# Gated delta-rule attention and experts on one core: keys and queries stored as feature rows by the projections

## The reference

```python
q = (x @ Wq).reshape(B, T, H, DK);  k = (x @ Wk)...;  v = (x @ Wv)...
x1, x2 = x[..., :d], x[..., d:]                       # d = DK // 2
rotary = concatenate([x1 * c + x2 * s, -x1 * s + x2 * c])
qr = l2norm(rotary(q, cos, sin)) * scale              # one set of angles per head and mode
kr = l2norm(rotary(k, cos, sin))
def step(S, inp):                                     # scanned over T, for every mode, batch and head
    q_t, k_t, v_t, b_g, b_beta = inp
    S = S * exp(b_g)[..., None, None]
    kv = einsum('mbhk,mbhkv->mbhv', k_t, S)
    dv = (v_t[None] - kv) * b_beta[..., None]
    S = S + k_t[..., :, None] * dv[..., None, :]
    o_t = einsum('mbhk,mbhkv->mbhv', q_t, S)
    return (S, o_t)
o = einsum('tmbhv,hm->bthv', ys, softmax(mode_logits))
x = x + (o * gate).reshape(B, T, H * DV) @ Wo
x = x + ffn(layernorm(x))                             # grouped top-2 of 8 experts
```

## Time and profile before

| | us |
|---|---|
| three timed runs | 4,367.66, 4,371.86, 4,394.44 (median 4,371.86) |
| the profiled execution (its span) | 4,385.0 |
| PE, DVE, ACT, POOL busy | 3,813.9, 3,552.6, 2,905.5, 380.0 |
| projections, tables | 14.9 to 274.6, 275 to 351 |
| recurrence, experts | 351 to about 3,890, 3,893 to 4,385 |

### The profile page before, as it was taken

The page is one execution under the profiler, slowest core; times in us unless marked ns, Lnnn a source line. Parts: engine busy times, 40 slices in busy tenths (PEclk is TensorE's granted clock), DMA queues, the critical chain, the costliest instruction groups (busy, mean ns, idle before and its releaser), DMA issues. The chain is left out here.

```text
span 4385.0 us, 193447 instructions
## 1 busy us (share of the span) xinstructions
PE 3813.9 (87%) x85713; PEld 3121.1 (71%) x85713; DVE 3552.6 (81%) x6909; ACT 2905.5 (66%) x9768; POOL 380.0 (9%) x220
## 2 busy tenths in 40 slices
PE   5513898999999999998999899999998999979999
PEld 2203787788778878777877778777777787766666
DVE  5676898888889988888898889889898988835665
ACT  5743677777677777777776767777677777744443
POOL 1230010000001000000000001000000000000000
PEclk8756899999899999999999989999999999989999
DMA  4664122222222222222221222232222222121110
GB/s 115 166 173 118 49 57 76 57 57 62 70 57 57 69 69 60 62 53 68 57 66 48 75 57 57 59 77 65 53 58 68 66 56 61 45 67 32 34 34 8
DMA packets 311716, 289.21 MB, mean 66 GB/s; under 512 B 137816, under 2 KB 250336, under 8 KB 308832
## 3 DMA queue, kind: packets, MB, share of 16 engines
q1 hardware_dynamic: 310880, 276.83, 24.5%
HBM read 215.92 MB, written 60.82 MB: 63 GB/s over the span
## 5 line engine op out<-in xcount | busy, mean ns | idle before, releaser
L922 DVE TENSOR_TENSOR run_EL<-run_XL 128x30 f32<-128x30 f32 (+14 forms) x1920 | 643.4, 335 | 66.0
L923 DVE TENSOR_TENSOR run_XL<-run_XL,run_EL 128x30 f32<-128x30 f32 (+14 forms) x1920 | 637.3, 332 | 66.0
L1059 PE MATMUL run_SP<-run_KP 64*32 64x128 f32 x8192 | 581.4, 283 | 21.7 <-DVE run_KP L909 12.2
L992 POOL TENSOR_TENSOR run_DB<-run_DB,run_below 128x1024 f32<-128x1024 f32 x128 | 306.5, 2395 | 3213.9 <-DVE run_KP L909 1758.5
L795 ACT ACTIVATE run_DB<-run_DB,run_col 128x64 f32<-128x64 f32 x2048 | 541.4, 350 | 4.7 <-POOL run_DB L992 1.0
L885 DVE TENSOR_TENSOR run_SC<-run_SP,run_DB 128x512 f32<-128x512 f32 x512 | 341.0, 685 | 248.9 <-ACT run_DB L795 156.3
L1059 PEld LDWEIGHTS run_SP<-run_KP 64*32 64x32 f32 x8192 | 426.5, 111 | 94.5 <-issue 68.1
L802 ACT ACTIVATE run_KD<-run_PR,run_col 128x64 f32<-128x64 f32 x2048 | 481.9, 329 | 17.0 <-PE run_PR L1078 9.1
L808 ACT ACTIVATE run_R<-run_KS,run_col 128x64 f32<-128x64 f32 x1792 | 417.1, 325 | 83.2 <-PE run_KS L1086 83.0
L1063 PE MATMUL run_SP<-run_KP 64*32 64x64 f32 x8192 | 413.9, 231 | 8.6 <-issue 8.6
L815 ACT ACTIVATE run_Sdec<-run_S,run_decay 128x64 f32<-128x64 f32 x1536 | 416.3, 372 | 0.0
(11 more groups left out here) (200 smaller groups left out, 7523.7 us busy)
## 6 DMA issues: line engine op xcount, KB each, us to landing
run_DB<-G_s SPq DMA_DIRECT2D x512, 128.0 KB, 2.9
run_EG<-EG_s SPq DMA_DIRECT2D x128, 512.0 KB, 6.7
KQ_s<-proj_win SPq DMA_DIRECT2D x32, 768.0 KB, 7.5
run_win<-KQ_s SPq DMA_DIRECT2D x64, 384.0 KB
run_tab<-TAB_s SPq DMA_DIRECT2D x64, 256.0 KB, 7.0
run_V<-V_s SPq DMA_DIRECT2D x128, 128.0 KB, 3.1
V_s<-proj_vv SPq DMA_DIRECT2D x64, 128.0 KB, 3.1
TAB_s<-tab_tab SPq DMA_DIRECT2D x64, 128.0 KB, 2.4
```

The costliest lines, as they stand in the source:

```text
L922: v.link(dve.tensor_tensor(e, bcast(XL[:, r + 1:, r], 2, done), bcast(XL[:, r, 0:done], 1, rows), ALU.mult))
L923: less = dve.tensor_tensor(XL[:, r + 1:, 0:done], XL[:, r + 1:, 0:done], e, ALU.subtract)
L1059: pe.matmul(out[64 * e:64 * e + C, p].rearrange("p (z u) i -> p z (u i)", z=2), KP[f, key, p, t0:t1], KP[f, kq, p, t0:t0 + SPAN], start=Tr ...
```

## The change

- **Projections.** `win`, its negated columns and POOL's program are gone. DVE writes the normalised keys and queries into `unit` (two batches deep) with as many multiplications as before. Two batches later, `flush` transposes two heads per tile on PE (8 transposes of 128 x 128), ACT copies one of the heads from PSUM into `kqF` and DVE the other; one store of 2 MB a batch puts `kqF` into `KQ_s`, now by feature rows. The loop over batches has two more turns, for the flushes of the last two. V goes out in 2 stores a batch, G and EG in 3. The PSUM banks of q, k and v become a ring of three.
- **Tables.** A third plane holds the negative sines: one more ACT instruction and 4 more stores per head (96 in all).
- **Recurrence.** The four turns on PE and ACT's four copies are gone. `kqT` holds two sequences and is loaded from `KQ_s` by six DMAs per sequence (1 MB), at the head of SP's step. The minus of the rotation comes from the table's third plane. V is read in runs of 64 floats instead of 512. The pipeline starts one step later (-2 instead of -3). Keys 2 and 3 stand in other places on PE; keys 4 to 7 and the exponentials of "next" on ACT. merge(0,1) waits for the last step's merges instead of the turns; DVE's rotations wait for the load.

```diff
-    KQ_s = dram("KQ_s", (H, B, 128, NT, 2 * WIN))
-    V_s = dram("V_s", (H, B, SPAN, SUPER, DV))
+    KQ_s = dram("KQ_s", (B, 2 * DK, H, T))
+    V_s = dram("V_s", (B, SPAN, NT, 2, H, DV))
...
-    TAB_s = dram("TAB_s", (H, 2, 2, HALF, PAIRS, T))
+    TAB_s = dram("TAB_s", (H, 3, 2, HALF, PAIRS, T))
...
-            for b in range(B + 1):
+            for b in range(B + 2):
                 for i in range(NT):
                     if b < B:
                         tile(b, i)
-                    if b:
+                    if 1 <= b <= B:
                         after(b - 1, i)
+                    if b >= 2:
+                        flush(b - 2, i)
...
-                    for i in range(NT):
-                        sp.dma_start(KQ_s[:, b, :, i, :].rearrange("h p e -> p h e"), win[:, i, :, :]).then_inc(put_k, 16)
...
+                    if b >= 2:
+                        sp.wait_ge(fill_a, H // 2 * (b - 1))
+                        sp.wait_ge(fill_v, H // 2 * (b - 1))
+                        sp.dma_start(KQ_s[b - 2], kqF[:, b % 2]).then_inc(put_k[b % 2], 16)
...
+                def flush(b, i):
+
+                    if i == 0:
+                        pe.wait_ge(k_unit, b + 1)
+                        pe.wait_ge(q_unit, b + 1)
+                    for u, filled in enumerate((fill_a, fill_v)):
+                        h = 2 * i + u
+                        if H * b + h >= 2:
+                            pe.wait_ge(filled, H // 2 * b + i)
+                        for t in range(NT):
+                            last = pe.transpose(FB[u][:, 128 * t:128 * t + 128],
+                                                unit[:, b % 2, t, h].rearrange("p z f -> p (z f)"), ident[:, :])
+                        last.then_inc(pe_f, 1)
...
+                    act.copy(kqF[:, b % 2, 2 * i, :], FB[0][:, :]).then_inc(fill_a, 1)
...
+                    dve.tensor_copy(kqF[:, b % 2, 2 * i + 1, :], FB[1][:, :]).then_inc(fill_v, 1)
...
-                            for k in range(2):
+                            for k in range(3):
                                 sp.dma_start(TAB_s[h, k, e, :, q::2, :], tab[at:at + 32, u, k]).then_inc(put[u], 16)
...
+                    act.activation(tab[:, u, 2], ang[:, u], ACT.Sin, scale=-1.0).then_inc(done, 1)
...
-        STEPS = range(-3, NSEQ)
+        STEPS = range(-2, NSEQ)
...
-                     ["turn 0"], ["keys 2"], ["turn 1"], ["keys 3"], ["next 1"], ["turn 2"], ["next 2"], ["turn 3"]]
...
+                     ["keys 2"], [], ["keys 3"], [], ["next 1"], [], ["next 2"], []]
...
+                def load_kq(n):
+
+                    both = KQ_s[n % B, :, n // B, :].rearrange("(z f) t -> f z t", z=2)
+                    for e in range(2):
+                        rows = slice(64 * e, 64 * e + DK)
+                        sp.dma_start(kqT[rows, n % 2, 0::2, :], both).then_inc(l_kq, 16)
+                        for half in range(2):
+                            at, other = 64 * e + HALF * half, HALF * (1 - half)
+                            sp.dma_start(kqT[at:at + HALF, n % 2, 1::2, :], both[other:other + HALF]).then_inc(l_kq, 16)
...
-                                sp.dma_start(tab[at:at + HALF, k], TAB_s[h, k, e]).then_inc(l_tab, 16)
+                                sp.dma_start(tab[at:at + HALF, k], TAB_s[h, k + (k and half), e]).then_inc(l_tab, 16)
...
+                                     V_s[n % B, :, :, :, n // B, :].rearrange("t i c v -> t (i c) v")).then_inc(l_v, 16)
...
-                        act.copy(kqT[:, r, :], PR[1][:, :]).then_inc(act_t, 1)
...
-                        dve.wait_ge(act_t, 4 * (b + 1))
+                        dve.wait_ge(l_kq, 96 * (b + 1))
...
-                        else:
-                            pe.wait_ge(act_t, 4 * min(k + 3, NSEQ))
+                        elif k:
+                            pe.wait_ge(act_m, 6 * k)
...
```

More of the change, by code:

```diff
@@ L228, in in_order, with nothing @@
                         begin(b + 1)
+        def nothing(*place):
+            pass
         with nc.Block() as block:
@@ L263, in _ @@
[L263 removed]
+                for b in range(B + 2):
+                    if b < B:
+                        sp.wait_ge(xt_copied, b + 1)
+                        sp.dma_start(XN_s[b], xT[:, b % 2]).then_inc(put_x[b % 2], 16)
+                        if b + 3 < B:
+                            sp.wait_ge(xt_done, b + 1)
+                            load(b + 3)
+                    if 1 <= b <= B:
+                        sp.wait_ge(gt_done, 3 * b)
+                        for u, rows in enumerate((gt, gt2)):
+                            sp.dma_start(G_s[b - 1, u], rows[:, :]).then_inc(put_g, 16)
+                        sp.dma_start(EG_s[b - 1], egt[:, :]).then_inc(put_g, 16)
+                    if b < B:
+                        sp.wait_ge(freed, item(b, NT - 1, VALUE) + 1)
+                        for c2 in range(2):
+                            sp.dma_start(V_s[b, :, :, c2].rearrange("t i h v -> t i (h v)"),
+                                         vv[64 * c2:64 * c2 + 64, b % 2].rearrange("t i h v -> t i (h v)")).then_inc(put_v[b % 2], 16)
+                    if b >= 2:
+                        sp.wait_ge(fill_a, H // 2 * (b - 1))
+                        sp.wait_ge(fill_v, H // 2 * (b - 1))
+                        sp.dma_start(KQ_s[b - 2], kqF[:, b % 2]).then_inc(put_k[b % 2], 16)
@@ L313, in after @@
                     last.then_inc(sums, 1)
-                in_order(begin, tile, after, lambda b: None)
+                def flush(b, i):
[10 more added lines that the diff above has]
+                        last.then_inc(pe_f, 1)
+                in_order(begin, tile, after, flush, nothing)
             @block.scalar
@@ L384, in end @@
                     act.activation(ez[:, b % 2], z[:, b % 2], ACT.Exp, scale=-1.0).then_inc(logs_out, 1)
-                in_order(begin, tile, after, end)
+                in_order(begin, tile, after, flush, end)
             @block.vector
@@ L629, in recurrence @@
         EG = sb("EG", [128, PAIRS, T])
-        win = sb("win", [128, NT, 2 * WIN])
-        kqT = sb("kqT", [128, 4, T])
+        kqT = sb("kqT", [128, 2, 4, T])
         tab = sb("tab", [128, 4, PAIRS, T])
@@ L839, in prepare_part @@
                         exponential(k + 2, i)
-                    if kind == "turn" and real(k + 3):
-                        turned(k + 3, i)
                 for k in STEPS:
@@ L1007, in _ @@
                 token_rows = PR[0][:, :].rearrange("p (z a f) -> p z a f", z=2, a=PAIRS)
-                def transposes(t, r):
-                    if r == 0:
-                        pe.wait_ge(l_win, 16 * (t + 1))
-                        if t >= 3:
-                            pe.wait_ge(act_m, 6 * (t - 2))
-                        elif t:
-                            pe.wait_ge(act_t, 4 * t)
-                    else:
-                        pe.wait_ge(act_t, 4 * t + r)
-                    off = WIN * (r // 2) + HALF * (r % 2)
-                    for i in range(NT):
-                        for e in range(2):
-                            last = pe.matmul(PR[1][64 * e:64 * e + 64, 128 * i:128 * i + 128], win[:, i, off:off + DK],
-                                             ident[:, :], start=True, stop=True)
-                    last.then_inc(pe_t, 1)
                 def merge(k, m, g):
@@ L1147, in prepare_part @@
                         scores(k + 2, i)
-                    if kind == "turn" and real(k + 3):
-                        transposes(k + 3, i)
                 for k in STEPS:
```

213 lines of the change are left out of this document (86 added, 127 removed).

## The result

The changed kernel takes 4,514.3 us (median of 4 runs, 4,495.8 to 4,533.4), the kernel before beside it 4,369.8. The ratio is 1.0315, 95% interval 1.027 to 1.036: slower by about 140 us, where 4,400 us and 4,230 to 4,465 were forecast. Its profiled execution has a span of 4,519.5 us.

The account below looks back on a forecast made before the run. The prediction took a loop of PE and DVE waiting on each other as the bound. Loop +7, projections +5, tables +21 and start -5 gave +28 us on 4,371.9, so 4,400 us, range 4,230 to 4,465.

Parts of the forecast that it names:

- Projections, tables, start: Stretches outside the loop: projections +5 us, tables +21 us for 32 more stores, start of the recurrence -5 us.
- PE has at least 49.9 - 46.7 = 3.2 us a step with nothing to do: Recurrence loop: DVE's own work less PE's without turns; about 3 us idle was expected right ahead of merge(0,0).
- PE's lateness goes, and merges at the low clock take its place.: Recurrence loop: PE reaches merge(0,0) on time but idle, its clock drops, and the loop gains nothing.
- I take step 0's length plus 0.1 ... with 0 to +20 as the case's own bounds.: Loop term: step 0's 54.38 us plus 0.1 over 62 steps, +7 us in total.
- keys ... Their cost is 0.: Loop: moved keys and ACT's later next exponentials have cover, since DVE takes scores of b only next step; 0 us.
- First rival: Loop: PE keeps its clock, DVE has no wait at take 4, steps near 50 us; 4,120 us, chance 0.10.
- Second rival: Loop: PE comes no earlier, waits in the PE and ACT chain fill what turns leave; 4,393 us, chance 0.10.
- Third rival: Loop: kqT and V loads stall PE's merges, DVE waits 1 us a step longer; +62, 4,460 us, chance 0.20.

Follow-up runs that it names:

- the run with the old places: The changed kernel with keys and next exponentials on PE and ACT placed as in the kernel before, without turns; 4,412.7 us, ratio 1.011 to the kernel before.
- a fill: The changed kernel with eight transposes of the identity at each of the turns' four former places; 4,361.2 us, ratio 0.996 to the kernel before.
- the run with an eighth of them: The kernel before with one matmul of the eight of each turn left in, copies, loads and places unchanged; 4,377.8 us, ratio 0.9985.
- the fill of four: The changed kernel with 32 identity matmuls, four turns' worth, ahead of merge(0,0); 4,463.2 us, ratio 1.021 to the kernel before.
- the four-place fill: The changed kernel with eight identity matmuls at each of the turns' four former places; 4,354.8 us, ratio 0.997 to the kernel before.

## Why the prediction was wrong

- **Projections, tables, start.** Right within 7 us each. The stores of the tables went at 47.29 / 60 = 0.79 us each, near the 0.82 that I took.
- **"PE has at least 49.9 - 46.7 = 3.2 us a step with nothing to do", ahead of merge(0,0).** Right in the main: behind step 0 it waits for TM 49 times, 2.3 us on the mean, and 0.9 at score 3 on the mean of 52 waits. So not all of it falls in the one place.
- **"PE's lateness goes, and merges at the low clock take its place."** Right in kind: 1.92 and 3.62 us for the merges, 4.52 us at take 4, as in rows 6. But the two idle times of rows 7 are no rule: behind 3.03 us the first merge at 1,812 us ran at full clock.
- **"I take step 0's length plus 0.1 ... with 0 to +20 as the case's own bounds."** This is the step that failed. The term measured +116 us instead of +7: a step lasts 56.28 us, not 54 to 54.6. (62 x 0.1 is 6.2, not 7, which changes nothing.) Step 0 of the kernel before is the mild form: its clock was back during merge(1,1), and DVE waited at take 4 "and nowhere else". In 43 of the 62 steps after, the clock came back only 2.4 to 5.8 us behind merge(1,1), which costs a second wait of 1.9 to 3.3 us; the changed kernel's own step 0 has one of 3.26. I had one step as a sample of a state that I forecast for sixty, and put the bound at 0.3 us a step, when the kernel before held steps with both waits, such as the one at 925 us with 4.68 and 3.10. What sets when the clock comes back from one step to the next, I can't tell from these runs.
- **"keys ... Their cost is 0."** Wrong too, by the run with the old places: the turns' missing work puts PE ahead of TM only together with these moves; with the old places the kernel was 1.1% slower than before, with the new ones 3.15%.
- **First rival** (50 us steps at a held clock): such steps exist, 50.44 us with a fill and one of 50.41 even in the kernel before, but none in the changed kernel, whose shortest is 51.68. **Second rival** (PE no earlier): near the truth for the turns' work alone, 3.0 us behind TM instead of 3.7 in the run with an eighth of them, not for the whole change. **Third rival** (issue stalls from the load): a real cost of 2.2 points with the fill of four; in the changed kernel itself the stalls of merge(1,0) are 3.6 us in all, and leaving the loads out gave nothing that can be told.
- The Trainium skill states on its page "TensorE: Matmul & The Clock Gate", section "Part 4: PE-mode transpose", that a transpose in that mode doesn't count for the clock as other PE work does. No run here settles it: filled with transposes the loop's clock was 0.93, with matmuls 0.94, and the times agree, but each of the four places holds only about 1.1 us of them between other work. The turns are plain matmuls, of which the rule doesn't speak, so it was no ground to give the first rival more chance.

## What to carry to other kernels

Work taken off an engine that two others wait for can make the kernel slower, if it then waits for its inputs in small pieces and comes out of these waits at a lower clock: ask what the engine will wait for next, and in what pieces. When one sample of a bad state is all that was looked at, price the state from the worst rows of it elsewhere in the trace, and not from that one. A step that is costed at nothing because something covers it, as the places of the keys were here, can still decide who comes early. And try a load away from the stretch where the critical engine issues many short instructions: with PE kept busy up to the merges the same six DMAs cost 2.2 points beside them, and with the four-place fill nothing that can be told behind chunk 5.

## What the runs showed of the hardware that was not expected

Matmuls whose result nobody reads sped the changed kernel up by 3.4%, since they held the granted clock (0.83 to 0.94). And PE's stalls that only "issue" explains followed the data loads beside them where PE was kept busy: 31.3 us in merge(1,0) with 1 MB of loads in that stretch, 6.3 us with the loads elsewhere. What makes these stalls, no run shows.
